# An attention kernel on one core: the mix for two steps behind every pair of maxima, instead of four steps behind every second pair

## The chip, the cores and the metric

The kernel runs on one NeuronCore of a Trainium2 chip. The metric is the device time of one execution in microseconds (us), from the kernel's start to its end. TensorE (PE) multiplies matrices, VectorE (DVE), ScalarE (ACT) and GpSimd (POOL) work element by element, SyncE (SP) issues the DMAs. Each engine runs its own list of instructions in order, and they wait for one another through semaphores.

## The reference

For 16 batches of 1024 tokens by 256 features, in fp32, with 8 heads of 64:

```python
h = _layernorm(x) * (1 + ca) + sa
q = h @ Wq.T;  kv = h @ Wkv_down.T;  k = kv @ Wk_up.T;  v = kv @ Wv_up.T
attn = softmax(einsum('bqhd,bkhd->bhqk', q, k) * scale)
x = x + ga * (einsum('bhqk,bkhd->bqhd', attn, v) @ Wo.T)
h = _layernorm(x) * (1 + cb) + sb
x = x + gb * (h @ weight.T + pooled(h) @ disha)
```

The modulations sa, ca, ga, sb, cb, gb are computed per batch from a conditioning vector; pooled(h) sums h over its four blocks of 64 features.

## The kernel before, in words

**Groups and steps.** The key projection is folded into the queries, so that all heads of a batch share one key matrix of 64 latent features. A batch has 8 groups (a pair of heads, half of the queries); a group has 8 steps, one for each tile of 128 keys. So a batch has 64 steps, and the whole kernel has 1024. In a step TensorE makes the scores of 128 keys against two times 512 queries (`scores`, L637 and L639, four matmuls, into the two halves of `ps_score`), ScalarE takes the exponential of each half into `probs` (L824), a ring of six steps, and GpSimd adds the step's probabilities to `prob_sum` (L991). The scores of half j wait for the exponential of half j of the step before, since it frees the bank.

**Maxima.** Softmax needs the row maxima of a group ahead of its scores. TensorE makes them 52 steps ahead, in every odd step (`maximum`, L665: two pairs of matmuls of 64 rows, one pair for each half of the keys, into both `ps_max` banks). VectorE reduces the two banks (L1139), and the next pair of maxima waits for that.

**The mix.** The product of the probabilities with the values (`mix`, L616) accumulates a group's eight steps in the bank `ps_mix`. A step has two fp32 matmuls of 128 rows and 64 columns, one for each half of the queries; they use the two column halves of the array side by side. The trace holds two records for each of them, so four records a step. `mixes` decides in which steps the mix runs, and how many steps it catches up on:

```python
def mixes(z, s):
    if s == 1 and z.has_o:
        for t in range(STEPS - MIXED, STEPS):
            mix(zo, t)
    if s > 1 and z.has_c and s % MIXED == 1:
        for t in range(s - MIXED - 1, s - 1):
            mix(z, t)
```

With MIXED = 4 that is in steps 1, 5, 9 and so on; step 1 mixes the last four steps of the batch before. In step 1 of every eight the mix completes a group, and ScalarE empties `ps_mix` (L855).

**Side work.** Everything else of a batch is cut into pieces that a table (`PLAN`) assigns to steps: projections (L602), transposes (L683, L698, L738), output projection (L731), feed-forward (L747), all in even steps; the transposed maxima (L707) in step 5 of every eight and the denominators (L717) in step 1 of every eight. The pieces use one bank, `ps_side`, in turn: a piece waits until the one before it has been read out by ScalarE or VectorE. In a step TensorE does, in this order, `scores`, `maximum`, `mixes`, `side_work`.

**ScalarE's rule.** It does a step's two exponentials and then reads out the step's side piece. The pieces of the steps that are 2 modulo 4 it leaves until after the next step's exponentials:

```python
late = z.has_c and s % MIXED == 2
for kind, i, b, w in z.at(s - 1) * (z.has_c and s % MIXED == 3) + z.at(s) * (not late):
```

**After a group.** The denominator goes through ScalarE (L897), DMAs, a reciprocal (L1093) and DMAs back to a multiplication on VectorE (L1105). `mixed_hi` (ScalarE, L845) and `mixed_lo` (VectorE, L1152) split the result for the output projection. The maxima of a group reach its scores through a DMA `query_m<-max_row`. For the last batch there is no next batch: no pieces of its input side, and no maxima after step 52.

Of the kernel before, what the change touches and what calls it, by code (L numbers as in the profile page):

```python
# [56 lines left out]
GROUPS = STEPS // NT  # L57

SPREAD_LAG, RECIP_LAG, OUT_LAG, BACK_LAG, MIX_LAG = 1, 2, 2, 3, 4
MIXED = 4  # L60


MAX_LAG = 52
# [144 lines left out]
@lru_cache(None)  # L208
def flagged(c):
    return Slot(c, c % 2, has_nn=c + 2 < B, has_n=c + 1 < B, has_c=0 <= c < B, has_o=c > 0)  # L210
# [31 lines left out]
def adaln_block(nc, x, wq, wkv_down, wk_up, wv_up, wo, weight, disha, c, wmod, out):  # L242
# [3 lines left out]
    with ExitStack() as ctx:  # L246
# [96 lines left out]
        def drained(eng, z, kind, i, wait=need, which=None):  # L343

            room, count = z.place(kind, i, which)
            wait(eng, side_drained[room], count + 1)
# [221 lines left out]
        def _(pe):  # L568
# [37 lines left out]
            def mix(z, s):  # L606

                g, k = divmod(s, NT)
                par = z.par
                if k == 0:  # L610

                    need(pe, group_evacuated, GROUPS * z.c + g)
                    if s == 0 and z.c == 0:
                        need(pe, side_drained[1], z.used(1))
                for j in range(2):
                    last = nc.tensor.matmul(ps_mix[j * R:j * R + R, :], values[par][:, k, :],  # L616
                                     probs[:, (STEPS * z.c + s) % RING, j * HALF:(j + 1) * HALF],
                                     start=(k == 0), stop=(k == NT - 1))
                if k == NT - 1:
                    last.then_inc(group_done, 1)  # L620
# [158 lines left out]
            def mixes(z, s):  # L779

                if s == 1 and z.has_o:
# [3 lines left out]
                    zo = Slot(z.o, 1 - z.par)  # L785
# [3 lines that stand above are left out]
                    if s == MIXED + 1:  # L789

                        for i in range(2):
                            drained(pe, flagged(z.c - 1), "values_t", i)
                    for t in range(s - MIXED - 1, s - 1):
                        mix(z, t)
# [12 lines left out]
        def _(act):  # L807
# [6 lines left out]
            def slot(z):  # L814
                for s in range(STEPS):
# [31 lines left out]
                    if s % NT == 1 and (z.has_o if s < NT else z.has_c):  # L847
# [4 lines left out]
                        if zg.has_o and p > half:  # L852
# [3 lines left out]
                                             ACT.Copy).then_inc(group_evacuated, 1)  # L856
                    late = z.has_c and s % MIXED == 2
                    for kind, i, b, w in z.at(s - 1) * (z.has_c and s % MIXED == 3) + z.at(s) * (not late):
                        room, count = z.place(kind, i, w)
# [384 lines left out]
```

## Time and profile before

| | |
|---|---|
| median of three runs | 3087.13 us (3084.59 to 3089.78) |
| profiled execution, its own time | 3085.94 us |
| its span, first to last instruction | 3083.8 us |
| TensorE matmul busy | 3026.8 us, 98% of the span |
| GpSimd busy | 2515.8 us, 82% |
| VectorE busy | 2022.8 us, 66% |
| ScalarE busy | 1679.1 us, 54% |
| mix, L616 (4096 records) | 935.4 us busy |
| scores, L637 and L639 (2048 records each) | 891.8 and 808.5 us busy |
| maxima, L665 (2048 records) | 376.2 us busy |

The time of the profiled execution is 2.1 us above its span: what lies around the first and last instruction. Records of TensorE overlap, since matmuls are pipelined; the distance between the starts of two records tells what the first cost, and its own length does not. "Idle" in brackets stands only where the engine has no record running. The trace of one batch is like that of the next, apart from the first and the last.

### The profile page before, as it was taken

To read this page: it belongs to the slowest core of one execution; us is meant where nothing else is said; L and a number is where in the kernel's file an instruction comes from. 1 tells how busy PE (TensorE), PEld (TensorE's weight loads), DVE (VectorE), ACT (ScalarE), POOL (GpSimd) and SP (SyncE) were. 2 spreads that over 40 slices of the span, in tenths; PEclk is the share of its full clock that TensorE was granted. 3 is DMA by queue.
4 is the path that set the end of the run, shared out by engine and by line. 5 is a ranking of instruction groups with operands and counts; after the bars stand their busy time and mean duration, and the time that the engine had idled before them with its cause. 6 is when DMAs were issued, how large, how long until landed. Compare 5 with 4: busy or idle time off the path is not lost. (4 is left out here: it accounts for less than half of the span.)

```text
span 3083.8 us, 44678 instructions
## 1 busy us (share of the span) xinstructions
PE 3026.8 (98%) x15138; PEld 1698.5 (55%) x15138; DVE 2022.8 (66%) x2452; ACT 1679.1 (54%) x3129; POOL 2515.8 (82%) x1520
## 2 busy tenths in 40 slices
PE   5999999999999999999999999999999999999998
PEld 4445555555555555555555555555555555555545
DVE  5566766667666666666666666666666666666664
ACT  3555555555555555555555555555555555555544
POOL 2888887888878888887888888888788888888787
PEclk9999999999999999999999999999999999999999
DMA  2111121121112111111111211111112111111111
GB/s 85 39 52 42 53 63 49 49 61 51 52 49 59 52 49 52 56 60 45 60 46 49 63 53 49 57 55 52 46 56 58 48 54 56 59 39 53 46 46 49
DMA packets 165346, 162.89 MB, mean 53 GB/s; under 512 B 62208, under 2 KB 113536, under 8 KB 165120
## 3 DMA queue, kind: packets, MB, share of 16 engines
q1 hardware_dynamic: 165120, 160.05, 17.8%
q8 instruction: 121, 1.98, 0.3%
q14 instruction: 105, 0.86, 0.1%
HBM read 74.40 MB, written 17.33 MB: 30 GB/s over the span
## 5 line engine op out<-in xcount | busy, mean ns | idle before, releaser
L991 POOL TENSOR_TENSOR prob_sum<-prob_sum,probs 128x1024 f32<-128x1024 f32 x768 | 1849.7, 2408 | 382.6 <-ACT probs L824 311.9
L1139 DVE TENSOR_REDUCE neg_max<-ps_max 128x1 f32<-128x1024 f32 x1024 | 1204.1, 1217 | 326.1 <-PE ps_max L665 322.1
L824 ACT ACTIVATE probs<-ps_score 128x512 f32<-128x512 f32 x2048 | 1113.1, 597 | 520.0 <-PE ps_score L639 489.5
L616 PE MATMUL ps_mix<-probs,values 128*64 128x512 f32 x4096 | 935.4, 598 | 0.8 <-ACT probs L824 0.8
L637 PE MATMUL ps_score<-query,key_hi 128*128 128x512 f32 x2048 | 891.8, 435 | 16.9 <-ACT probs L824 8.1
L639 PE MATMUL ps_score<-query_m,key_lo 128*128 128x512 f32 x2048 | 808.5, 395 | 0.0
L616 PEld LDWEIGHTS ps_mix<-probs,values 128*64 128x64 f32 x4096 | 271.3, 136 | 532.8 <-issue 531.6
L637 PEld LDWEIGHTS ps_score<-query,key_hi 128*128 128x128 f32 x2048 | 384.6, 188 | 269.2 <-ACT probs L824 101.6
L639 PEld LDWEIGHTS ps_score<-query_m,key_lo 128*128 128x128 f32 x2048 | 386.8, 189 | 46.5
L665 PE MATMUL ps_max<-key_hi,query 64*128 64x512 f32 x2048 | 376.2, 445 | 7.0 <-DVE neg_max L1139 6.9
L991 POOL TENSOR_TENSOR prob_sum<-probs 128x1024 f32<-128x1024 f32 x128 | 307.0, 2398 | 71.6 <-ACT probs L824 71.6
L665 PEld LDWEIGHTS ps_max<-key_hi,query 64*128 64x128 f32 x2048 | 152.9, 185 | 191.6 <-issue 167.8
L855 ACT ACTIVATE mixed<-ps_mix 128x512 f32<-128x512 f32 x128 | 76.4, 597 | 328.2 <-PE ps_mix L616 328.2
L928 ACT ACTIVATE max_row<-ps_side 8x128 fp32r<-8x128 f32 x128 | 34.2, 267 | 382.3 <-PE ps_side L707 382.3
L1172 DVE TENSOR_TENSOR query<-ps_side,query 64x512 fp32r<-64x512 f32 x248 | 170.7, 688 | 95.8 <-ACT query L865 92.7
L1105 DVE TENSOR_TENSOR mixed<-mixed,recip 128x512 f32<-128x512 f32 x127 | 163.9, 1291 | 99.6 <-DMA recip<-recip_scratch 97.5
L1202 DVE TENSOR_TENSOR x_mid<-ps_side,x_mid 128x256 f32<-128x256 f32 x121 | 51.0, 422 | 218.7 <-PE ps_side L731 218.7
L865 ACT ACTIVATE query<-ps_side 64x512 fp32r<-64x512 f32 x248 | 146.8, 592 | 83.6 <-PE ps_side L602 80.6
L731 PE MATMUL ps_side<-w_out_lo,mixed_hi 128*128 128x256 f32 x480 | 134.6, 280 | 0.0
L731 PE MATMUL ps_side<-w_out_hi,mixed_lo 128*128 128x256 f32 x480 | 134.4, 280 | 0.0
L731 PE MATMUL ps_side<-w_out_hi,mixed_hi 128*128 128x256 f32 x480 | 133.8, 279 | 0.0
L1212 DVE TENSOR_TENSOR x_mid<-ps_side,x_mid 128x512 f32<-128x512 f32 x60 | 41.5, 691 | 139.9 <-PE ps_side L747 139.8
(182 smaller groups left out, 2612.2 us busy)
## 6 DMA issues: line engine op xcount, KB each, us to landing
query_m<-query SPq DMA_DIRECT2D x128, 256.0 KB, 2.4
query_m<-query SPq DMA_DIRECT2D x256, 128.0 KB, 2.6
recip<-recip_scratch SPq DMA_DIRECT2D x254, 128.0 KB, 2.9
x_in<-in_L_attn_x_dram SPq DMA_DIRECT2D x32, 512.0 KB, 4.7
x_mid<-in_L_attn_x_dram SPq DMA_DIRECT2D x64, 256.0 KB, 3.1
out_dram<-x_mid SPq DMA_DIRECT2D x64, 256.0 KB, 2.2
denoms<-recip SPq DMA_DIRECT2D x508, 1.0 KB, 1.7
gates<-gates_scratch SPq DMA_DIRECT2D x16, 256.0 KB, 4.5
```

What stands on the lines that cost most here:

```text
L616: last = nc.tensor.matmul(ps_mix[j * R:j * R + R, :], values[par][:, k, :], probs[:, (STEPS * z.c + s) % RING, j * HALF:(j + 1) * HALF], s ...
L637: nc.tensor.matmul(ps_score[j], key_hi[z.par][:, k * P:(k + 1) * P], group_queries(g)[:, j, :], start=True, stop=False)
L639: nc.tensor.matmul(ps_score[j], key_lo[z.par][:, k * P:(k + 1) * P], query_m[:, g % 2, j * HALF:(j + 1) * HALF], start=False, stop=True).t ...
L665: last = nc.tensor.matmul(ps_max[j][:, half * HALF:(half + 1) * HALF], query[rows, 2 * p + j, qt * P:(qt + 1) * P], key_hi[kpar][rows, hal ...
L731: last = nc.tensor.matmul(side[:, 0:D], mp[:, p, j * P:(j + 1) * P], wp[:, pair, :], start=(q == 0), stop=(q == len(products) - 1))
L824: nc.scalar.activation(probs[:, (STEPS * z.c + s) % RING, half * HALF:(half + 1) * HALF], ps_score[half], ACT.Exp, scale=SCALE).then_inc(e ...
L855: nc.scalar.activation(mixed_block(zg.par, p, half), ps_mix[:, :], ACT.Copy).then_inc(group_evacuated, 1)
L865: nc.scalar.activation(query[j * R:(j + 1) * R, 2 * p + j, half * HALF:(half + 1) * HALF], side[j * R:(j + 1) * R, :], ACT.Copy).then_inc( ...
L991: nc.gpsimd.tensor_tensor(out=total[:, :], in0=before, in1=probs[:, now % RING, :], op=ALU.add).then_inc(adds_done, 1)
L1105: nc.vector.tensor_tensor(raw, raw, recip[:, :], ALU.mult).then_inc(group_mixed, 1)
L1139: nc.vector.tensor_reduce(neg_max[:, col:col + 1], ps_max[j][:, :], AX_X, ALU.max, negate=True).then_inc(maxima_done, 1)
L1172: last = nc.vector.tensor_tensor(query[(1 - j) * R:(2 - j) * R, 2 * p + j, cols], side[j * R:(j + 1) * R, :], query[j * R:(j + 1) * R, 2 * ...
```

## The change

One constant. The mix runs in all odd steps, each time for two steps; step 1 takes the last two steps of the batch before. The same constant stands in ScalarE's rule: a step modulo 2 is never 2 or 3, so no piece is left until after the next exponentials any more.

```diff
-MIXED = 4
+MIXED = 2
```

**TensorE**, two places of the middle of the program: an odd step with maxima that had no mix before, and one that ends a group (L717 is the denominator). A line such as `64x512 x8` counts one per fp32 matmul, so eight are four steps of mix.

```order
 L639 MATMUL ps_score<-query_m,key_lo 128x512
 L665 MATMUL ps_max<-key_hi,query 128x512 x4
+L616 MATMUL ps_mix<-probs,values 64x512 x4
 L637 MATMUL ps_score<-query,key_hi 128x512
 L639 MATMUL ps_score<-query_m,key_lo 128x512
```

```order
 L639 MATMUL ps_score<-query_m,key_lo 128x512
 L665 MATMUL ps_max<-key_hi,query 128x512 x4
-L616 MATMUL ps_mix<-probs,values 64x512 x8
+L616 MATMUL ps_mix<-probs,values 64x512 x4
 L717 MATMUL ps_side<-prob_sum,ones_cols 32x256 x4
 L637 MATMUL ps_score<-query,key_hi 128x512
```

Half of each long mix has moved to the odd step in front of it, between the maxima and the next scores. The matmuls are the same in number and shape.

**ScalarE**, the order from step 41 to step 46 of a batch (L890 reads out the values of step 42), before:

```order
L855 ACTIVATE mixed<-ps_mix 128x512
L897 ACTIVATE recip<-ps_side 128x256
L824 ACTIVATE probs<-ps_score 128x512 x4
L890 ACTIVATE values<-ps_side 128x256
L824 ACTIVATE probs<-ps_score 128x512 x2
L865 ACTIVATE query<-ps_side 64x512 x2
```

and in the changed kernel:

```order
L855 ACTIVATE mixed<-ps_mix 128x512
L897 ACTIVATE recip<-ps_side 128x256
L824 ACTIVATE probs<-ps_score 128x512 x2
L890 ACTIVATE values<-ps_side 128x256
L824 ACTIVATE probs<-ps_score 128x512 x4
L865 ACTIVATE query<-ps_side 64x512 x2
```

The readout of step 42 now comes ahead of the exponentials of step 43. In a batch of the middle this concerns four pieces: the transposes of steps 18 and 58, and the values of steps 42 and 46.

## Rows read from the trace of the kernel before

**Rows 1.** Stretch of one batch: busy us per engine, TensorE clock, DMA.
```profile
292.00:480.00 188.00, 188.00 (x947) 105.70 (x944) 126.17 (x153) 104.59 (x196) 157.60 (x95) 1.00 0.18 54
```

**Rows 2.** Timeline, batch 7, steps 43 to 45: start, length, engine, line, tiles.
```profile
1503.00 0.74 PE L665 MATMUL ps_max<-key_hi,query 64*128 64x512 f32 x4
...
1503.66 0.51 PE L637 MATMUL ps_score<-query,key_hi 128*128 128x512 f32 x1
...
1504.01 0.40 PE L639 MATMUL ps_score<-query_m,key_lo 128*128 128x512 f32 x1
...
1507.12 0.73 PE L665 MATMUL ps_max<-key_hi,query 64*128 64x512 f32 x4
...
1507.79 3.65 PE L616 MATMUL ps_mix<-probs,values 128*64 128x512 f32 x16
...
1508.27 0.14 PEld L616 LDWEIGHTS ps_mix<-probs,values 128*64 128x64 f32 x2 [0.28 <-issue]
...
1510.41 0.14 PEld L616 LDWEIGHTS ps_mix<-probs,values 128*64 128x64 f32 x2 [0.28 <-issue]
...
1511.37 0.27 PE L707 MATMUL ps_side<-ident,neg_max 128*8 128x128 f32 x1
```

**Rows 3.** Timeline, batch 15, step 61: a mix followed directly by scores.
```profile
3043.40 3.65 PE L616 MATMUL ps_mix<-probs,values 128*64 128x512 f32 x16
...
3046.99 0.50 PE L637 MATMUL ps_score<-query,key_hi 128*128 128x512 f32 x1
...
3047.32 0.39 PE L639 MATMUL ps_score<-query_m,key_lo 128*128 128x512 f32 x1
```

**Rows 4.** View of waits, PE, 105 to 2890 us: total, times, longest.
```profile
PE ps_score L637 <- DMA query_m<-max_row: 3.5, 5, 1.4
PE ps_score L637 <- ACT probs L824: 2.8, 10, 0.3
```

**Rows 5.** View of waits, PE, from 2890 us.
```profile
PE ps_score L637 <- ACT probs L824: 5.0, 16, 0.7
```

**Rows 6.** Timeline, batch 15, steps 8 and 9: a wait for exponentials.
```profile
2897.92 0.40 PE L639 MATMUL ps_score<-query_m,key_lo 128*128 128x512 f32 x1
2898.59 0.50 PE L637 MATMUL ps_score<-query,key_hi 128*128 128x512 f32 x1 [0.28 <-ACT probs L824]
```

**Rows 7.** Timeline, batch 0: GpSimd sums, and the denominator that waits for them.
```profile
88.66 12.38 POOL L991 TENSOR_TENSOR prob_sum<-prob_sum,probs 128x1024 f32<-128x1024 f32 x5
...
101.09 0.64 PE L717 MATMUL ps_side<-prob_sum,ones_cols 128*32 128x256 f32 x8 [2.08 <-POOL prob_sum L991]
```

**Rows 8.** Timeline, batch 7, step 17: the maxima.
```profile
1425.01 0.73 PE L665 MATMUL ps_max<-key_hi,query 64*128 64x512 f32 x4 [1.33 <-DVE neg_max L1139]
```

**Rows 9.** Timeline, batch 7, step 60: side work right after scores.
```profile
1551.07 0.40 PE L639 MATMUL ps_score<-query_m,key_lo 128*128 128x512 f32 x1
1551.34 0.50 PE L602 MATMUL ps_side<-h_hi,w_in_hi 128*128 128x512 f32 x1
1551.68 0.40 PE L602 MATMUL ps_side<-h_lo,w_in_hi 128*128 128x512 f32 x1
```

**Rows 10.** Timeline, batch 7, steps 8 and 9: one room handed over.
```profile
1402.74 1.06 ACT L824 ACTIVATE probs<-ps_score 128x512 f32<-128x512 f32 x2
...
1402.87 0.75 DVE L1196 SCALAR_TENSOR_TENSOR h_lo<-ps_side,mod,h_whole 128x512 fp32r<-128x512 f32 x1 [0.54 <-ACT h_whole L886]
...
1405.09 0.64 PE L717 MATMUL ps_side<-prob_sum,ones_cols 128*32 128x256 f32 x8
```

**Rows 11.** Timeline, batch 7, steps 45 and 47: maxima against their reduction.
```profile
1509.28 2.35 DVE L1139 TENSOR_REDUCE neg_max<-ps_max 128x1 f32<-128x1024 f32 x2
...
1514.01 0.74 PE L665 MATMUL ps_max<-key_hi,query 64*128 64x512 f32 x4
```

**Rows 12.** Timeline, end of batch 15: GpSimd sums, and the last denominator.
```profile
3039.39 15.21 POOL L991 TENSOR_TENSOR prob_sum<-prob_sum,probs 128x1024 f32<-128x1024 f32 x6 [2.96 <-ACT probs L824]
...
3054.67 0.14 PEld L714 LDWEIGHTS ps_side<-prob_sum,ones_cols 128*64 128x64 f32 x2 [0.29 <-POOL prob_sum L991]
```

## The prediction, made before the run

> **What bounds the kernel now.** First the busy shares by stretch. In a batch of the middle TensorE is busy for all 188.00 of 188 us, at a granted clock of 1.00 (2.4 GHz), while GpSimd, the next, has 157.60 [rows 1]. So a full batch ends when TensorE has gone through its list. Second, the waits of TensorE: between 105 and 2890 us, in 2785 us, the two largest come to 3.5 and 2.8 us [rows 4]. Hardly any wait is left to remove. What decides is therefore how far apart its matmuls start, and a busy row hides that. So third the timeline, read by the starts.
>
> Take the maxima of step 43. They start at 1503.00, the scores follow at 1503.66 and their second matmul at 1504.01 [rows 2]. Step 45 has maxima too, but a mix behind them: 1507.12 to 1507.79, 0.67 us, so the maxima cost the same in front of a mix as in front of scores. The mix runs until L707 starts at 1511.37, 3.58 us for four steps, eight pairs of records. Inside it the weight loads step along with the pairs: from 1508.27 to 1510.41 are five pairs, 0.43 us each [rows 2]. Eight pairs at 0.43 would be 3.44 us. The mix costs 0.14 to 0.15 more than its pairs: the **seam**, some 0.05 at its first pair (1507.79 to 1508.27 is 0.48) and some 0.10 behind its last.
>
> **The change, part by part.**
>
> *Added seams.* The pairs stay the same in number. But the mix was in 256 pieces (16 batches of 16) and is now in 512, so 256 seams are added. Is a seam paid when scores follow, not L707 or L717? There is one such place, in step 61 of the last batch, which has no maxima: 3043.40 to 3046.99 is 3.59 us, the same seam, and the second matmul of the scores then comes 0.33 later (3047.32), as it does behind maxima (0.35) [rows 2, 3]. So nothing more is paid behind the mix than was paid behind the maxima before, and nothing less. A seam lies on TensorE itself, with nothing beside it that could hide it. Bounds for one: 0 (all of it hidden when another kind of matmul follows, against both rows) and 0.15. I take 0.15, which every long mix of the trace shows: 256 x 0.15 = **+38.4 us**. A piece of two steps then takes 4 x 0.43 + 0.15 = 1.87 us.
>
> The Trainium skill has a rule that speaks against this change: on the page "TensorEngine Tiling (Array Packing)", section Tiling Modes, changing the tiling mode drains the engine. The page "TensorE: Matmul & The Clock Gate", section Single matmul latency, gives (398 + N)/2.4 ns for a matmul alone; less its gap of 216 ns back to back, that is an estimate of 163 ns for one drain at N = 512. The change adds one change of mode per added piece, so by these pages it would cost 256 x 0.163 = 42 us; the rows say 38, and they decide.
>
> *Two seams in batch 0 are free.* There GpSimd is late: its five sums run without a break from 88.66 to 101.04, and the denominator of step 9 waits for them until 101.09 (2.08 us idle) [rows 7]. TensorE has the same work behind it at that point in both orders. The pieces added in steps 3 and 7 fall in that wait: -0.3 us. Whatever else gets faster there is swallowed in the same way.
>
> *The maxima's DMA.* Scores wait five times for `query_m<-max_row`, 3.5 us in all [rows 4]. The transposed maxima (step 5 of eight) are now made ahead of half a mix that used to come before them, and the other half stands in step 7, so the DMA gets 1.7 us more. The longest wait was 1.4: all go, **-3.5 us**.
>
> *VectorE.* The maxima of step 17 in batch 7 waited 1.33 us for the reduction [rows 8]. From step 15 to step 17 there is now a piece of mix more: -1.3. The other way round, from step 1 to step 3 of every four, 1.7 us are lost (3.58 less 1.87). The tightest regular place is step 47: the reduction ends at 1511.63, the maxima start at 1514.01, 2.38 us later [rows 11]; 0.66 is left, so no new wait.
>
> *ScalarE.* Its readouts of steps 18, 42, 46 and 58 now precede the next exponentials. The cover is the new piece of 1.87 us in steps 19, 43, 47 and 59, behind which the scores that need those exponentials stand. The readout of step 8 already works like this, and is longer: its exponentials of step 9 run until 1403.80, with L717 at 1405.09 [rows 10]. So I cost it at nothing. Without that cover it would be the rival below. It also ends one delay: in step 60 of fifteen batches the side work starts 0.27 behind the scores and its second matmul 0.34 later, where 0.23 each is usual [rows 9], since the piece of step 58 was read out late. 15 x 0.15 = -2 us.
>
> *A room handed over sooner.* The piece of step 8 must be read out before L717 of step 9. VectorE ends that at 1403.62, L717 starts at 1405.09: 1.47 us of room [rows 10]. All of that chain hangs on exponentials of step 8, which now come 1.87 later, while L717 moves by one seam. 1.47 - 1.87 + 0.15 is 0.25 short. Between 0 (the neighbours of this place have a little more room) and 15 x 0.25 = 4 us; I take **+1**.
>
> *The end.* Batch 15 waits for exponentials 16 times, 5.0 us idle [rows 5]. Most are two steps without side work in a row; the mix isn't between them, and they stay. In the last steps the mix comes between some of them. But GpSimd's six sums run without a break from 3039.39 to 3054.60, and the last denominator's weights load at 3054.67 right behind them [rows 12]. So what is saved behind 3039 is mostly not seen: -1 us.
>
> Sum: 38.4 - 0.3 - 3.5 - 1.3 - 2 + 1 - 1 = +31.3 us. It is made against the profiled execution, 3085.94 us (a span of 3083.8 and 2.1 around it): 3117.2. The median of the three runs is 1.2 above that execution, so the forecast for the median is **3118 us**. A measurement of this kernel can tell about 0.2%, 6 us, from no change.
>
> **The rivals.**
>
> A. *Seams, and no relief.* The small waits come back in other places, and the hand-over of step 9 costs its 4 us everywhere: 3087.1 + 38.4 + 4 = 3129.5. For it: GpSimd and the DMAs keep their load. Against it: every wait named above gets 1.7 us. Chance 0.12.
>
> B. *Seams, and more relief.* All waits behind 105 us go, those of batch 15 too. A wait that shows 0.28 idle costs more: 2897.92 to 2898.59 is 0.67 where 0.23 is usual [rows 6], 0.44, and some 0.1 on the matmul behind it. The 26 waits for exponentials (10 and 16) would so give back 7.8 idle + 26 x 0.26 = 15 us [rows 4, 5], beyond the forecast: 3103. Against it: most have no mix between the two steps. Chance 0.07.
>
> C. *ScalarE late.* If the new piece does not cover the readouts, each of the four steps in 15 batches costs as a wait of [rows 6] does, 0.54 us: 33 us more, 3151. It decides as soon as readout and exponentials together take longer than maxima and mix. Against it [rows 10]. Chance 0.04.
>
> D. *The other side: no seam in front of scores.* If TensorE takes the weights of the scores into the array while the last pair of the mix still streams, and the first pair's 0.05 is hidden as well, only the relief is left: 3087.1 - 7 = 3080, faster. The point from which it decides is a seam under 0.03 us. For it: inside a mix the loads are hidden behind the running pairs, which start every 0.43 [rows 2]. Against it: [rows 3], a mix with scores behind it, and 0.15 paid. The Trainium skill has a rule for it, on the page "TensorE: Matmul & The Clock Gate", section Part 3 (The mechanism): a weight load that doesn't conflict is pulled ahead of matmuls in flight. In this trace that holds inside the mix and not at its end. Chance 0.04. A seam of which most is hidden, so that relief and cost cancel within 0.2%, has 0.03.
>
> **How the numbers follow.** The forecast has 0.70, with a range of its own of 3108 to 3126, for relief between 4 and 16 us and a seam of 0.14 to 0.16. The whole range takes in A and B: 3102 to 3130; C, D and the seam mostly hidden lie outside. Slower by over 0.2%: 0.70 + 0.12 + 0.07 + 0.04 = 0.93. Within 0.2%: 0.03. Faster: 0.04.
>
> **What the new profile would show.** L616 in rows of eight records, 1.87 us from its start to the next start, in odd steps alike; L637 starting some 0.10 us later behind the last pair than a further pair would. A batch of the middle longer by 16 x 0.15 = 2.4 us. No wait for `query_m<-max_row` at all. In step 9, L717 with no idle time or 0.25 us. VectorE's wait for the reciprocals before L1105 short. If batches of the middle keep their length, the seam was misread. If the wait of L637 for L824 grows beyond some 8 us in all, the cover on ScalarE failed.

## The result, and the profile after

The changed kernel takes 3121.9 us in the median of three executions, the kernel before, run beside it, 3088.3 us. A fourth execution of the changed kernel took 10177 us at a granted clock of 0.29 and is left out (with it the median is 3122.7). The ratio is 1.0107, with a 95% interval of 1.0094 to 1.0121: slower by some 33 us (29 to 37). The forecast was 3118 us, 31 us more. The profiled execution took 3121.9 us with a span of 3118.6, 34.8 us more than the span before.

The page of the changed kernel, its line on the engines and the groups of the mix and of the multiplication by the reciprocals (busy us, mean ns | idle before, and what ended it):

```profile
PE 3062.2 (98%) x15138; PEld 1678.3 (54%) x15138; DVE 2037.1 (65%) x2452; ACT 1677.2 (54%) x3129; POOL 2529.6 (81%) x1520
...
L616 PE MATMUL ps_mix<-probs,values 128*64 128x512 f32 x4096 | 991.6, 605 | 0.0
...
L1105 DVE TENSOR_TENSOR mixed<-mixed,recip 128x512 f32<-128x512 f32 x127 | 184.5, 1453 | 14.2 <-DMA recip<-recip_scratch 12.3
```

TensorE is as busy as before, 98%. The same 4096 records of the mix now cover 991.6 us instead of 935.4: the time went into TensorE's own list. (These 56 us hold some 18 that are not cost: the row of a piece reaches 0.07 us past the start of what follows, and there are 255 more such ends.) The view by stretch says the same of a batch of the middle (columns as in [rows 1]):

```profile
308.00:497.00 189.00, 188.96 (x942) 104.11 (x940) 126.58 (x153) 103.85 (x196) 157.25 (x95) 1.00 0.18 53
```

From the start of batch 1 to the start of batch 14 are 2463.16 us (255.41 to 2718.57), 2436.03 before (249.94 to 2685.97): 27.1 us more in 13 batches, 2.09 each. The prediction gave 2.4 as a sign; that is the 16 seams alone, and the relief comes off it.

The timeline of batch 7, steps 45 and 47, against [rows 2] (start, length):

```profile
1525.43 0.73 PE L665 MATMUL ps_max<-key_hi,query 64*128 64x512 f32 x4
1526.10 1.94 PE L616 MATMUL ps_mix<-probs,values 128*64 128x512 f32 x8
1527.97 0.27 PE L707 MATMUL ps_side<-ident,neg_max 128*8 128x128 f32 x1
...
1530.60 0.73 PE L665 MATMUL ps_max<-key_hi,query 64*128 64x512 f32 x4
1531.27 1.08 PE L616 MATMUL ps_mix<-probs,values 128*64 128x512 f32 x4
```

and its weight loads:

```profile
1526.10 0.20 PEld L616 LDWEIGHTS ps_mix<-probs,values 128*64 128x64 f32 x4 [0.37 <-issue]
1526.58 0.14 PEld L616 LDWEIGHTS ps_mix<-probs,values 128*64 128x64 f32 x2 [0.29 <-issue]
1527.01 0.14 PEld L616 LDWEIGHTS ps_mix<-probs,values 128*64 128x64 f32 x2 [0.28 <-issue]
```

A piece of two steps runs from 1526.10 to 1527.97, 1.87 us, with 0.48 for its first pair and 0.43 for the next: four pairs at 0.43 are 1.72, and the seam is 0.15, as long as that of a piece of four steps. It is paid in front of scores just as well, here in step 61 of the last batch, against [rows 3]:

```profile
3079.23 1.94 PE L616 MATMUL ps_mix<-probs,values 128*64 128x512 f32 x8
3081.10 0.50 PE L637 MATMUL ps_score<-query,key_hi 128*128 128x512 f32 x1
3081.43 0.40 PE L639 MATMUL ps_score<-query_m,key_lo 128*128 128x512 f32 x1
```

1.87 us, then 0.33 to the second matmul of the scores.

What relief there was is in TensorE's waits between 105 and 2920 us, against [rows 4]:

```profile
PE ps_score L637 <- ACT probs L824: 2.8, 10, 0.3
PE ps_score L637 <- DMA query_m<-max_row: 1.4, 1, 1.4
PE ps_side L717 <- DVE h_lo L1196: 0.3, 1, 0.3
```

Four of five waits for the DMA are gone, that of batch 0 is not. The ten waits for exponentials are the same, the wait for the maxima [rows 8] is gone, and one for the readout of step 8's piece is new. VectorE's idle time in front of its 127 instructions of L1105 fell from 99.6 us (97.5 of it 73 waits for the DMA) to 14.2 (12.3 of it 7 waits): the reciprocals got the time foreseen, but nobody had waited for VectorE there.

### The profile page after: what moved, and what is told of

Its sections match the earlier page's. It is cut to its first block, busy times and chain, and to the rows that moved or that the text cites. A ratio compares the mean times of both kernels' runs of the same rounds, so it can differ in the third digit from the quotient of the medians.

```text
span 3118.6 us, 44678 instructions
## 1 busy us (share of the span) xinstructions
PE 3062.2 (98%) x15138; PEld 1678.3 (54%) x15138; DVE 2037.1 (65%) x2452; ACT 1677.2 (54%) x3129; POOL 2529.6 (81%) x1520
## 4 chain that ended last, share of the span: by engine, by line
PE 94%; POOL 2%; DVE 1%; ACT 1%; issue 1%; DMA 0%; SPq 0%; POOLq 0%; ACTq 0%; DVEq 0%
PE ps_mix L616 30%; PE ps_score L637 18%; PE ps_score L639 15%; PE ps_max L665 11%; PE ps_side L602 7%; PE ps_side L731 5%; PE ps_side L747 3%; PE ps_side L717 2%; POOL prob_sum L991 2%; PE ps_side L707 1%; PE ps_side L683 1%; PE ps_side L738 1%; ACT probs L824 1%; PE ps_side L698 0%; DVE neg_max L1139 0%
## 5 line engine op out<-in xcount | busy, mean ns | idle before, releaser
L616 PE MATMUL ps_mix<-probs,values 128*64 128x512 f32 x4096 | 991.6, 605 | 0.0
L637 PE MATMUL ps_score<-query,key_hi 128*128 128x512 f32 x2048 | 892.2, 436 | 13.4 <-ACT probs L824 7.1
L639 PE MATMUL ps_score<-query_m,key_lo 128*128 128x512 f32 x2048 | 810.1, 396 | 0.0
L637 PEld LDWEIGHTS ps_score<-query,key_hi 128*128 128x128 f32 x2048 | 384.5, 188 | 378.1 <-issue 263.2
L616 PEld LDWEIGHTS ps_mix<-probs,values 128*64 128x64 f32 x4096 | 248.5, 136 | 480.0 <-issue 480.0
L639 PEld LDWEIGHTS ps_score<-query_m,key_lo 128*128 128x128 f32 x2048 | 386.6, 189 | 46.1
L1105 DVE TENSOR_TENSOR mixed<-mixed,recip 128x512 f32<-128x512 f32 x127 | 184.5, 1453 | 14.2 <-DMA recip<-recip_scratch 12.3
L1152 DVE TENSOR_TENSOR mixed_lo<-mixed,mixed_hi 128x1024 fp32r<-128x1024 f32 x62 | 95.4, 1538 | 57.8 <-ACT mixed_hi L845 57.8
L1196 DVE SCALAR_TENSOR_TENSOR h_lo<-ps_side,mod,h_whole 128x512 fp32r<-128x512 f32 x61 | 45.8, 751 | 133.2 <-ACT h_whole L886 133.2
L602 PE MATMUL ps_side<-h_hi,w_in_hi 128*128 128x512 f32 x310 | 122.6, 395 | 1.5 <-DVE h_lo L1196 1.5
```

Source lines behind the costliest of these rows:

```text
L602: last = nc.tensor.matmul(side[:, :], w[:, f, rows], h[:, f, cols], start=(j == 0), stop=(j == len(products) - 1))
L637: nc.tensor.matmul(ps_score[j], key_hi[z.par][:, k * P:(k + 1) * P], group_queries(g)[:, j, :], start=True, stop=False)
L639: nc.tensor.matmul(ps_score[j], key_lo[z.par][:, k * P:(k + 1) * P], query_m[:, g % 2, j * HALF:(j + 1) * HALF], start=False, stop=True).t ...
L1105: nc.vector.tensor_tensor(raw, raw, recip[:, :], ALU.mult).then_inc(group_mixed, 1)
```

## The experiments

The seam theory: the change costs 0.15 us for every piece of mix that it adds, on TensorE alone, and where the pieces stand hardly matters. The rivals: new waits through the moved halves, and ScalarE's changed order. The experiments all start from the kernel before, but for the last.

**A piece cut in place.** The mix of four steps is cut in two within its step, around the maxima. Nothing moves to another step.

```diff
-                    maximum(z, s)
-                    mixes(z, s)
+                    mixes(z, s, 0)
+                    maximum(z, s)
+                    mixes(z, s, 1)
...
-                    for t in range(s - MIXED - 1, s - 1):
+                    for t in (range(s - 5, s - 3), range(s - 3, s - 1))[part]:
                         mix(z, t)
```

(Step 1 splits the last four steps of the batch before in the same way.)

> The kernel before, with each mix of four steps cut in two inside its own step: two steps of mix, the maxima, two steps of mix. No piece moves to another step, so no engine waits for anything longer or shorter than before. Seam theory (a piece of mix costs 0.15 us beyond its pairs wherever it stands): some 253 pieces more, 38 us, 3126 us. Variant of it (only a change to the full array is dear, a change between two half modes is cheap): well under that, the first pair's 0.05 only, about 13 us. Rival (the changed kernel is slower since pieces stand in other steps and waits moved): no change, 3088 us.

Measured: ratio 1.0127 (1.0112 to 1.0142), 3125.1 us in the median, +39 us. The timeline of batch 7, step 45:

```profile
1524.74 1.94 PE L616 MATMUL ps_mix<-probs,values 128*64 128x512 f32 x8
1526.60 0.73 PE L665 MATMUL ps_max<-key_hi,query 64*128 64x512 f32 x4
1527.27 1.94 PE L616 MATMUL ps_mix<-probs,values 128*64 128x512 f32 x8
1529.13 0.27 PE L707 MATMUL ps_side<-ident,neg_max 128*8 128x128 f32 x1
```

Both pieces take 1.86 to 1.87, the one in front of the maxima too. A change from the mode of the mix (tiles of 128 by 64) to that of the maxima (64 by 128) is no cheaper than one to the full array. In batches 1 to 14 the stretch from one step's scores to the next is 0.15 us longer in all 16 steps that have a mix. The 39 us came with no half moved to another step, so the moved halves can't be what makes the change slow. The intervals of this run and of the changed kernel overlap, so that 39 is more than 33 isn't shown. Against the expectation, some waits did fall: those for the DMA from 3.5 us to 0.6, and the one for the maxima [rows 8] is gone. The second matmul of step 60 still came late, as in [rows 9].

**ScalarE's rule alone.**

```diff
-                    late = z.has_c and s % MIXED == 2
-                    for kind, i, b, w in z.at(s - 1) * (z.has_c and s % MIXED == 3) + z.at(s) * (not late):
+                    late = False
+                    for kind, i, b, w in z.at(s):
```

> The kernel before, MIXED = 4, with ScalarE's rule as the change leaves it: no piece is left until after the next exponentials. Seam theory: no piece of mix is added, so at most the waits of steps 19, 43, 47 and 59, which have no mix here; step 60 loses its delay of 0.15. Between -2 and +5 us, 3086 to 3093 us. Rival (the cost of the change comes through ScalarE's order): +20 us or more, 3108 us and up, with waits of L637 for L824 in those steps.

Measured: ratio 1.0002 (0.9992 to 1.0011), no difference. TensorE's waits over the whole kernel, those that the rule could have touched:

```profile
PE ps_score L637 <- ACT probs L824: 8.8, 29, 0.7
PE ps_max L665 <- DVE neg_max L1139: 8.0, 6, 3.5
```

Before they were 8.1 us in 27 places and 6.9 in 5: less than 2 us in a kernel of 3084. ScalarE's order carries nothing. Neither is there a cover here: without the new piece of mix the scores behind steps 19 and 59 come 0.08 us late, and nothing is lost in steps 43 and 47. The late matmul of step 60 is gone too: in batch 7 its first two side matmuls start 0.23 and 0.23 apart, where [rows 9] has 0.27 and 0.34.

**Three pieces a group.** Half of the added pieces.

```diff
-                    for t in range(STEPS - MIXED, STEPS):
+                    for t in range(STEPS - 2, STEPS):
                         mix(zo, t)
-                if s > 1 and z.has_c and s % MIXED == 1:
+                if s > 1 and z.has_c and s % 8 in (1, 5, 7):
...
-                    for t in range(s - MIXED - 1, s - 1):
+                    for t in range(s - (5 if s % 8 == 5 else 3), s - 1):
                         mix(z, t)
```

> Three pieces a group instead of two (before) or four (changed): four steps of mix in step 5 of every eight, two in step 7, two in step 1. ScalarE's rule as before. Seam theory: 128 pieces added, 128 x 0.15 = 19 us, less a few us of relief: 3102 to 3108 us, half of what the change costs. Rival (the cost comes from where the halves stand, from waits): not in proportion to the pieces.

Measured: ratio 1.0056 (1.0041 to 1.0071), 3103.1 us in the median, +17 us, half of what the change costs (1.0107). The cost goes with the number of pieces.

**One step of mix in every step.**

```diff
-                if s > 1 and z.has_c and s % MIXED == 1:
+                if s > 1 and z.has_c:
...
-                    for t in range(s - MIXED - 1, s - 1):
-                        mix(z, t)
+                    mix(z, s - 2)
```

(Steps 0 and 1 mix steps 62 and 63 of the batch before in the same way.)

> One step of mix in every step: 1024 pieces in place of 256. 256 more stand behind maxima, at 0.15 each: 39 us. 512 stand in even steps, behind scores and in front of side work or scores: they also bring the entry (0.09) and the slower second matmul behind the exit (0.10) that maxima pay anyway, 0.345 each: 177 us. Seam theory: 3088 + 216 = 3304 us. Rival (what costs is the length of the stretch without mix, so an even spread is best): faster than the changed kernel, under 3120 us.

Measured: ratio 1.0655 (1.0631 to 1.0678), 3288.3 us, +202 us; an even spread is the worst of all, as the seam theory has it. Its sum was 216. The largest two of TensorE's waits:

```profile
PE ps_side L707 <- DVE query L1169: 14.4, 61, 1.6
PE ps_side L717 <- DVE query L1169: 12.7, 60, 0.2
```

27 us are waits for a readout that the theory had not counted: side work of even steps starts later by a piece of mix, and the piece behind it in the odd step no longer finds the bank free. Since the sum was too high even so, the piece of an even step costs less than the 0.345 us assumed. The waits for exponentials went from 8.1 us to 0.3, since the mix now stands between all steps; with the 0.26 that each of these 27 costs besides [rows 6] that is 15 us of relief. With the span 204.1 longer, 39 of it for the pieces behind maxima and 27 for the new waits, 512 pieces have 204.1 - 39 - 27 + 15 = 153 us, 0.30 each. The trace tells where the difference to 0.345 lies. In batches 1 to 14 such a piece adds 0.34 to 0.36 us beyond its pairs where projections, output projection or feed-forward follow it, but 0.19 in nine of the ten even steps whose side work is transposes. (Steps 20 and 60, which started late before, add less.) Behind transposes the scores had paid for their slower second matmul already, as here in step 8 of batch 7 of the changed kernel (0.34 from L637 to L639):

```profile
1417.40 0.60 PE L683 MATMUL ps_side<-ident,x_in 128*128 128x128 f32 x4
1417.84 0.50 PE L637 MATMUL ps_score<-query,key_hi 128*128 128x512 f32 x1
1418.18 0.40 PE L639 MATMUL ps_score<-query_m,key_lo 128*128 128x512 f32 x1
```

So where a piece stands does matter, against the seam theory as it was put above: behind maxima it adds one change of tile mode, between matmuls of the full array two.

**The denominators in the mode of the mix.** What is the seam? In the trace before, the very last piece reaches L714 after 3.48 us (3051.61 to 3055.09), while all others reach L707 or L717 after 3.58. L714 is a matmul of the mix's own tile mode. So all denominators were made in that way:

```diff
-                        for q in range(QUARTERS if z.has_c else 0):
-                            last = nc.tensor.matmul(side[q * QR:(q + 1) * QR, 0:QC], ones_cols[:, 0:QR],
-                                                    prob_sum[i % 2][:, q * QC:(q + 1) * QC], start=True, stop=True)
+                        for j in range(2):
+                            last = nc.tensor.matmul(side[j * R:(j + 1) * R, :], ones_cols[:, :],
+                                                    prob_sum[i % 2][:, j * HALF:(j + 1) * HALF], start=True, stop=True)
...
-                            nc.scalar.activation(prob_total[:, 0:QC], side[:, 0:QC], ACT.Copy).then_inc(side_drained[room], 1)
+                            nc.scalar.activation(prob_total[:, :], side[:, :], ACT.Copy).then_inc(side_drained[room], 1)
```

(The DMAs that spread the denominators take them from where they now stand.)

> The kernel before, with the denominators of all batches made as the last one is: two fp32 matmuls of 64 columns of the array and 512 of the sums, the mode of the mix, in place of four of 32 columns and 256. The copy behind them on ScalarE is twice as long. In the trace of the kernel before the last mix reaches its L714 in 3.48 us, all others reach L717 or L707 in 3.58. Mode theory (the 0.10 behind a piece is the price of a change of the array's tile mode, the 0.05 of its first pair too): start to start from the last pair of the mix to the denominator 0.42 in all 128 places, and no 0.05 inside the denominator; it then takes 1.72 us to the second matmul of the scores, against 1.43 for L717, +37 us, 3125 us. Rival (the 0.10 is the end of an fp32 piece, whatever follows): 0.52 us there, and +50 us, 3138 us.

Measured: ratio 1.0122 (1.0103 to 1.0141), 3126.1 us, +37 us. Batch 7, step 9 (L713 are the denominators here):

```profile
1426.55 3.65 PE L616 MATMUL ps_mix<-probs,values 128*64 128x512 f32 x16
1430.04 1.03 PE L713 MATMUL ps_side<-prob_sum,ones_cols 128*64 128x512 f32 x4
1431.00 0.50 PE L637 MATMUL ps_score<-query,key_hi 128*128 128x512 f32 x1
1431.33 0.39 PE L639 MATMUL ps_score<-query_m,key_lo 128*128 128x512 f32 x1
```

The mix reaches the denominators after 3.49, and in all 127 places without a wait the distance from its last record (which starts 0.007 behind the first of its pair) is 0.42, not 0.52. The two pairs of the denominators take 0.96 until the scores start: 0.43 for the first, with no 0.05, and 0.53 for the second, which now pays the 0.10. From 1430.04 to 1431.33 are 1.29 us and the last pair of the mix takes 0.43: 1.72, as the mode theory said. In batches 1 to 14 of the trace every such step is 0.29 us longer; 128 of them are 37 us. (The profiled execution was 5 us above the median of this kernel.)

One rival is left to look at: by the program's declarations the mix is fp32, the scores and the maxima are fp32r (the profile prints f32 for both). It isn't the type that makes the 0.10 behind the last pair, since L717 and L713 are both fp32 and only L717 pays it. The two differ also in the columns that stream (256 and 512); no run separates that from the tile mode. Entering the feed-forward (L747, fp32, full array) from scores costs nothing extra either: 0.23 and then 0.22 us a matmul. But the second matmul of the scores comes 0.10 late behind transposes too (the rows above), where the type changes and the tiles stay 128 by 128. So, as far as these runs separate it, what goes with the change of tile mode is the seam of the mix, 0.10 and 0.05 us; the slower second matmul of the scores goes with more than that. The Trainium skill's rule on the page "TensorEngine Tiling (Array Packing)", section Tiling Modes, that a change of mode drains the engine, agrees with this run; the run shows the delay, 0.10 us, and not the drain itself.

**The changed kernel with the old rule of ScalarE.**

```diff
-                    late = z.has_c and s % MIXED == 2
+                    late = z.has_c and s % 4 == 2
```

(and `s % 4 == 3` in the line behind it).

> The changed kernel with ScalarE's rule as before (the pieces of the steps that are 2 modulo 4 are left until after the next exponentials). Seam theory: the pieces of mix are those of the changed kernel, so its time within 3 us, 3122 to 3126 us; the 0.15 us of step 60 don't come back either if it is the new piece of mix in step 59 that gives the room, and do (+2 us) if it is the rule. Rival (ScalarE's order carries a part of the cost): nearer to the kernel before, 3110 us or less.

Measured: ratio to the kernel before 1.0098 (1.0081 to 1.0115), 3119.0 us in the median, 3 us under the expected range. The interval overlaps that of the changed kernel; by their spans the two differ by 1.2 us (3117.4 and 3118.6). The late matmul of step 60 doesn't come back: the piece of mix in step 59 gives the room by itself, as the rule did by itself in the run with ScalarE's rule alone.

No version that beats the kernel before came out of this. The theory asks for fewer pieces than two a group, one for all eight steps. That was not tried: the ring of probabilities would have to hold ten steps instead of six, and the maxima and denominators of steps 1 and 5 lose the mix that covers their readouts.

## Why the prediction was right

**The added seams** (+38.4) are nearly the whole cost. The size of one held: 0.15 for 1.87 us pieces, in front of L707, L717 and scores alike. There are 255 more, not 256: in the last batch the piece of step 63 and that of the next step 1 touch, and form one row of 16 records. To three digits a piece takes 1.868 us and a pair 0.429, so a seam is 0.151, and 255 of them are 38.5. That the cause is the change of tile mode stands in the prediction only as a rule that it quotes; the experiment on the denominators bears it out.

**The free seams in batch 0** (-0.3). The prediction said that what gets faster there is swallowed by GpSimd. It was: L717 starts 0.21 us later than before, as the first scores of the kernel already do (0.22), with two pieces more in front of it. And there was more: TensorE ran ahead, and then stood still for longer (against [rows 7]).

```profile
88.91 12.33 POOL L991 TENSOR_TENSOR prob_sum<-prob_sum,probs 128x1024 f32<-128x1024 f32 x5
```

```profile
92.83 1.94 PE L616 MATMUL ps_mix<-probs,values 128*64 128x512 f32 x8
101.30 1.08 PE L717 MATMUL ps_side<-prob_sum,ones_cols 128*32 128x256 f32 x8 [6.53 <-POOL prob_sum L991]
102.31 0.79 PE L637 MATMUL ps_score<-query,key_hi 128*128 128x512 f32 x1
102.90 0.63 PE L639 MATMUL ps_score<-query_m,key_lo 128*128 128x512 f32 x1
103.33 0.63 PE L637 MATMUL ps_score<-query,key_hi 128*128 128x512 f32 x1
```

Both sums end at about the same time, 101.04 and 101.24. But the wait is 6.53 us instead of 2.08, and the matmuls behind it start 0.43 us apart where 0.23 is usual. The view by stretch tells why (the seventh number is the granted clock):

```profile
97.00:101.00 4.00, 0.00 (x0) 0.00 (x0) 0.00 (x0) 0.00 (x0) 3.86 (x2) 0.61 0.00 0
101.00:105.00 4.00, 3.70 (x15) 1.82 (x16) 0.00 (x0) 1.56 (x3) 2.56 (x2) 0.54 0.01 1
105.00:109.00 4.00, 4.00 (x19) 1.55 (x17) 1.62 (x2) 1.70 (x4) 3.76 (x2) 1.00 0.01 1
```

While TensorE stood still the clock fell to 0.50, which is 1.2 GHz, and it was still there when TensorE started again (in single microseconds it is 0.50 from 98 to 104 and 1.00 from 105; the stretches above mix the two). Before, the same stretches had 1.00. From the start of L717 to the first scores of step 11 are 4.18 us (101.30 to 105.48) instead of 2.70 (101.09 to 103.79): this cost 1.5 us. The prediction had nothing for it. But it isn't clearly the change's. In the run with ScalarE's rule alone, where no piece of mix is added, the same wait is 3.9 us, and the clock was at 0.50 as well when L717 started; so it was in all six experiments, with waits of 3.6 to 5.7 us. How long this wait gets differs between executions, and why is open.

**The maxima's DMA** (-3.5) gave 2.1 of idle time, and 2.8 at the starts of the scores. The step that failed: the longest wait was 1.4 and the DMA gets 1.7 more, so all go. In batch 0 the scores of step 24 come later by more than that (138.81 to 142.77, where the transposed maxima come later by 2.1), and wait 1.4 us all the same. From the issue of the DMA to the scores are 5.8 us (136.93 to 142.77), before 3.9 (134.95 to 138.81). It is issued right behind a load of 512 KB, `x_in`, that lands 5.1 us after its issue before and 7.0 after. Before, the scores started ahead of that landing, so that the load holds up the DMA isn't shown. The distance in the program was right; that the transfer takes as long as before was an assumption. Why it takes longer there stays open. In the sum the prediction also put waits at their idle time, though its rival B says that a wait costs more than it shows.

**VectorE** (-1.3): held; the wait of step 17 in batch 7 is gone, and gave 1.6 at the starts, for the same reason. The tightest place of the other kind, step 47, has 0.97 left, 0.66 was foreseen.

**ScalarE** (0, and -2 for step 60): held. The readouts cost nothing, by the rule's own experiment, and hardly anything without the cover of 1.87 us either. Step 60 of batch 7:

```profile
1570.00 0.40 PE L639 MATMUL ps_score<-query_m,key_lo 128*128 128x512 f32 x1
1570.23 0.40 PE L602 MATMUL ps_side<-h_hi,w_in_hi 128*128 128x512 f32 x1
1570.47 0.39 PE L602 MATMUL ps_side<-h_lo,w_in_hi 128*128 128x512 f32 x1
```

0.23 and 0.24, where [rows 9] has 0.27 and 0.34. This holds in 14 batches, 2.0 us; batch 0 had no such delay before. The reason given, the late readout, holds by the rule's own experiment; but it is half of the story, since in the changed kernel with the late readout restored the delay stayed away too.

**The room handed over** (+1): the mechanism held, the size was larger. Batch 7, step 9, against [rows 10]:

```profile
1421.91 0.64 PE L717 MATMUL ps_side<-prob_sum,ones_cols 128*32 128x256 f32 x8 [0.31 <-DVE h_lo L1196]
```

Batch 7 idles 0.31 us (0.25 by the sum) and starts L717 0.38 late, and 13 others start it 0.10 late: 1.7 us.

**The end** (-1): the last batch gave 0.8 beside its seams. The last denominator is bound by GpSimd, as foreseen, and TensorE now waits for it:

```profile
3084.87 3.65 PE L616 MATMUL ps_mix<-probs,values 128*64 128x512 f32 x16
3090.42 1.08 PE L714 MATMUL ps_side<-prob_sum,ones_cols 128*64 128x512 f32 x4 [1.89 <-POOL prob_sum L991]
```

With the terms as measured, by the starts in the two traces, the sum is 38.5 - 0.3 - 2.8 - 1.6 - 2.0 + 1.7 - 0.8, and 1.5 for the clock and 0.2 for the first scores: 34.4, and the span grew by 34.8. The forecast was +31.3: the parts that it missed are the clock (1.5), the hand-over (0.7) and the DMA (0.7), and smaller ones of both signs. These small terms compare one execution with one; the three of the changed kernel spread over 5.5 us, the four of the kernel before over 5.2. The seams are all that is well clear of this.

Of the rivals, A (no relief) and B (all waits go) are told apart by the waits: four of the DMA's and the one of the maxima went, and all those for exponentials between 105 and 2920 us stayed, as the forecast had it. C fell with the trace of the changed kernel, which has no new wait for exponentials, and the experiment on ScalarE's rule shows that it would not have come without the cover either. D fell with every trace: no seam is hidden in front of a matmul of another mode.

## What to carry to other kernels

Where one engine has no waits left, read the distance between starts rather than busy time, and count how often it changes between kinds of matmul: here a piece of the mix costs 0.15 us beside its work where it adds one change of tile mode (behind maxima), and 0.30 on average where it adds two (between matmuls of the full array), however long the piece is. Spreading work evenly over steps relieves waits, and is worth it only where there are waits; here it bought back some 7 us of waits and delays and brought 1.7 of another, for 39. A single wait that grows costs more than its length if TensorE's clock falls in it.

## What the runs showed of the hardware that was not expected

The seam of the mix has two parts, and both go with the change of tile mode: 0.10 us behind its last pair, 0.05 at its second pair. They are paid between tiles of 128 by 64 and 64 by 128 too (the piece cut in place), and not between two different products of the same mode, which follow each other at 0.42 us like two steps of the mix (127 places). Full-array scores pay in another way: a piece of mix starts 0.33 us behind their last matmul, where 0.23 is usual, and behind a piece their second matmul comes 0.34 after the first instead of 0.23; the latter is so behind transposes as well. And a standstill of 6.5 us took TensorE's granted clock from 1.00 to 0.50 (1.2 GHz), and so did those of 3.6 to 5.7 us in the same place in the experiments, where one of 2.1 us had left it at 1.00.
